# Projections with the bias in the weights' last row, and reciprocal roots by Newton steps on GpSimd

## The chip, the cores and the metric

The kernel runs on one core of a Trainium2 chip. The metric is the device time of one execution in microseconds (us); lower is better. PE is TensorE, DVE is VectorE, ACT is ScalarE, POOL is GpSimd, SP is SyncE, which here only issues DMAs.

## The reference, cut to what matters

The program is a whole two-layer model. The change lies in the first part of layer 0, a normalization, a feed-forward block on its result, and the projections of a recurrent attention:

```python
hs = layernorm(x)                       # 4096 tokens x 128; mean 0 over the 128 features
q = silu(hs @ Wq + bq)                  # 128 -> 16 heads x 64; the same for k and v
g = hs @ Wg + bg                        # 128 -> 1024, with silu
beta = sigmoid(hs @ Wb + bb)            # 16 heads; 4 more gates alike
q = q * rsqrt(sum(q * q, axis=-1) + 1e-6)   # per token and head; the same for k
```

The q, k and v that leave this stage are scaled per token and head: q and k by their reciprocal norms, k and v also by the root of beta.

## The kernel before, in words

The kernel is written engine by engine; each engine's instructions run in the order written, and semaphores order them between engines. Phases end with `end_phase`, where every engine waits for every other.

**Load stage and feed-forward block (0 to 203 us).** SP issues the loads. Those counted by `ld2` are the gate weights `wgate`, gate biases, small constants, the projection bias `bias_p` and the four weight matrices `wproj` (L1533 to L1539). DVE normalizes all 4096 tokens at once (L507 to L516), with `xnT` as scratch space, quantizes the result and the weights (L581 to L593), and then works through 16 pairs of token tiles. PE turns each tile of `xn`, ACT copies it to `xnT` (`keep_x`, L2077), and from there the gate logits are formed (L1811, L1814). POOL clears `bias3` and splits the bias into three bf16 parts (L1674 to L1681), which go through DRAM into three rows of `bias3`.

**Projections (203 to 506 us).** There are 32 tiles of 128 tokens, each with 4096 outputs in 8 PSUM banks. Per tile i:

- PE computes for each bank the f32 product (L1858) and adds the bias by a bf16 matmul of ones with the three bias rows (L1859). It reuses a bank when ACT has read the same bank of tile i-1.
- ACT evicts each bank through Silu (L2124), and squares q after bank 2 and k after bank 4 (L2130, L2133). After bank 2 it also takes the roots of the 32 sums of the tile before (L2128).
- DVE sums the squares per head (L2320, L2332), takes the reciprocals of the roots of tile i-1 (L2317) and multiplies q, k and v of tile i-1 in place by `prj_f`, one instruction on 128x3072 (L2325).
- POOL squares v (L1699) and multiplies the factors of k by the root of beta (L1693).
- SP stores the finished tile, 2 MB, to `proj_s` (L1556). `prj` has four slots, and ACT waits for the store of tile i-4.

DVE's order in turn i is: reciprocal (i-1), sum of q (i), multiply (i-1), sum of k (i), sum of v (i). The quotes from the other engines stand below.

Of the kernel before, what the change touches and what calls it, by code (L numbers as in the profile page):

```python
# [42 lines left out]
ROUNDER = 1.5 * 2 ** 22  # L43
TIES_DOWN = 1.0 - 2.0 ** -22
# [26 lines left out]
def layer_kernel(nc, a, out):  # L71

    ctx = ExitStack()
    with ctx:
        def sem(name):
            return ctx.enter_context(nc.semaphore(name))
# [21 lines left out]
        bias_s = nc.dram_tensor("bias_s", (3, 4 * HD), BF16, kind="Internal").ap()  # L98
# [32 lines left out]
        above_fa = sb("above_fa", [P, T * D], scope=s1)  # L131
# [15 lines left out]
        ones3 = sb("ones3", [P, P], BF16, scope=sW)  # L147
# [12 lines left out]
        bias3 = sb("bias3", [P, 4 * HD], BF16, scope=s2)  # L160
# [206 lines left out]
        v_prj = sem("v_prj")  # L367
        p_normed = sem("p_normed")
# [109 lines left out]
        bias_split, bias_out, bias_in, b_summed = bias_sems  # L478
# [25 lines left out]
        def layernorm(dve, c, src, dst, turned, layer):  # L504
# [11 lines left out]
            c.link(dve.tensor_tensor(dst[:, :, :], dst[:, :, :], rstd.unsqueeze(2).to_broadcast([P, T, D]), ALU.mult))  # L516

# [1004 lines left out]
        def _(sp):  # L1522
# [142 lines left out]
        def _(pool):  # L1665
# [11 lines left out]
            split.link(pool.tensor_copy(bias_h[:, 0, :], bias_p[:, :]))  # L1677
            split.link(pool.tensor_tensor(bias_r[:, 0, :], bias_p[:, :], bias_h[:, 0, :], ALU.subtract))
            split.link(pool.tensor_copy(bias_h[:, 1, :], bias_r[:, 0, :]))
            split.link(pool.tensor_tensor(bias_r[:, 1, :], bias_r[:, 0, :], bias_h[:, 1, :], ALU.subtract))  # L1680
            split.done(pool.tensor_copy(bias_h[:, 2, :], bias_r[:, 1, :]))  # L1681
# [8 lines left out]
            for i in range(T + 1):  # L1690
                if i >= 1:
                    pool.wait_ge(v_prj, i + 1)
                    pool.tensor_tensor(prj_f[:, i - 1, H0:2 * H0], prj_f[:, i - 1, H0:2 * H0], sb_tok[:, i - 1, :], ALU.mult).then_inc(p_sq, 1)  # L1693
                if i < T:
                    pool.wait_ge(p_silu, 8 * i + 6)
                    if i:
                        pool.wait_ge(p_red, 3 * i)
                    x = prj[:, i % 4, 2 * HD:3 * HD]
                    pool.tensor_tensor(prj_sq[:, 2, :], x, x, ALU.mult).then_inc(p_sq, 1)  # L1699
# [72 lines left out]
        def _(pe):  # L1772
# [32 lines left out]
            def gate_logits(p):  # L1805

                if p == 0:
                    pe.wait_ge(ld2, 144)
# [254 lines left out]
        def _(act):  # L2063
# [9 lines left out]
            def keep_x(p):  # L2073
# [3 lines left out]
                act.copy(xnT[:, 2 * P * p:2 * P * p + 2 * P], bank[0][:, 0:2 * P]).then_inc(xT_done, 1)  # L2077
# [40 lines left out]
            for i in range(T + 1):  # L2118
                if i < T:
                    if i >= 4:  # L2120
                        act.wait_ge(p_stored[i % 4], 16 * (i // 4))
                    for n in range(8):
                        act.wait_ge(p_mm, 8 * i + n + 1)
                        act.activation(prj[:, i % 4, 512 * n:512 * n + 512], bank[n], ACT.Silu).then_inc(p_silu, 1)  # L2124
                        if n == 2:
                            if i:
                                act.wait_ge(p_red, 3 * i - 1)
                                act.activation(prj_n[:, (i - 1) % 2, 1, :], prj_n[:, (i - 1) % 2, 0, :], ACT.Sqrt, bias=prj_eps[:, 0:1]).then_inc(p_std, 1)  # L2128
                            act.wait_ge(p_silu, 8 * i + 2)
                            act.activation(prj_sq[:, 0, :], prj[:, i % 4, 0:HD], ACT.Square).then_inc(p_sq_q, 1)  # L2130
                        if n == 4:
                            act.wait_ge(p_silu, 8 * i + 4)
                            act.activation(prj_sq[:, 1, :], prj[:, i % 4, HD:2 * HD], ACT.Square).then_inc(p_sq_q, 1)  # L2133
            act.wait_ge(p_red, 3 * T - 1)
            act.activation(prj_n[:, (T - 1) % 2, 1, :], prj_n[:, (T - 1) % 2, 0, :], ACT.Sqrt, bias=prj_eps[:, 0:1]).then_inc(p_std, 1)
# [117 lines left out]
        def _(dve):  # L2253
# [25 lines left out]
            for p in range(FP):  # L2279
# [8 lines left out]
                if p == FP - 2:  # L2288
                    dve.wait_ge(g_raw, 2 * FP)
                    dve.tensor_tensor(sb_tok[:, :, :], sb_tok[:, :, :], beta_row[:, 0:2 * H0:2].unsqueeze(1).to_broadcast([P, T, H0]), ALU.add).then_inc(b_summed, 1)  # L2290
                    dve.wait_ge(ld2, 144)
# [17 lines left out]
            pv_ = Count(dve, p_var)  # L2309
            for i in range(T + 1):  # L2310
# [4 lines left out]
                if i >= 1:  # L2315
                    dve.wait_ge(p_std, i)
                    prc.link(dve.reciprocal(prj_f[:, i - 1, 0:2 * H0], prj_n[:, (i - 1) % 2, 1, :]))  # L2317
                if i < T:
                    dve.wait_ge(p_sq_q, 2 * i + 1)
                    dve.tensor_reduce(prj_n[:, i % 2, 0, 0:H0], prj_sq[:, 0, :].rearrange("p (h d) -> p h d", d=DK), AX, ALU.add).then_inc(p_red, 1)  # L2320
                if i >= 1:
                    t = i - 1
                    dve.wait_ge(p_sq, 2 * i)
                    qkv3 = prj[:, t % 4, 0:3 * HD].rearrange("p (h d) -> p h d", d=DK)
                    dve.tensor_tensor(qkv3, qkv3, prj_f[:, t, :].unsqueeze(2).to_broadcast([P, 3 * H0, DK]), ALU.mult).then_inc(p_normed, 1)  # L2325
                if i < T:
                    for w, dst in ((1, prj_n[:, i % 2, 0, H0:2 * H0]), (2, vv[:, i, :])):
                        if w == 1:
                            dve.wait_ge(p_sq_q, 2 * i + 2)
                        else:  # L2330
                            dve.wait_ge(p_sq, 2 * i + 1)
# [284 lines left out]
```

## Time and profile before

| | |
|---|---|
| three runs | 3071.02 us median (3070.17 to 3073.48) |
| profiled execution | 3071.01 us |
| its span in the trace | 3069.2 us |
| load stage and feed-forward block | 0 to 203 us |
| projections | 203 to 506 us |
| busy of the span: PE, DVE, ACT, POOL | 86%, 75%, 52%, 45% |
| busy in 200 to 506 us: PE, DVE, ACT, POOL | 289, 234, 286, 92 us |

A busy share over the whole span mixes stages with different limits; for this change the stage of the projections and the load stage before it are to be read by themselves. The page's chain of work that ended last holds only about a fifth of the span and does not reach back to these stages. Spans on POOL are rough.

### The profile page before, as it was taken

To read this page: it belongs to the slowest core of one execution; us is meant where nothing else is said; L and a number is where in the kernel's file an instruction comes from. 1 tells how busy PE (TensorE), PEld (TensorE's weight loads), DVE (VectorE), ACT (ScalarE), POOL (GpSimd) and SP (SyncE) were. 2 spreads that over 40 slices of the span, in tenths; PEclk is the share of its full clock that TensorE was granted. 3 is DMA by queue.
4 is the path that set the end of the run, shared out by engine and by line. 5 is a ranking of instruction groups with operands and counts; after the bars stand their busy time and mean duration, and the time that the engine had idled before them with its cause. 6 is when DMAs were issued, how large, how long until landed. Compare 5 with 4: busy or idle time off the path is not lost. (4 is left out here: it accounts for less than half of the span.)

```text
span 3069.2 us, 68844 instructions
## 1 busy us (share of the span) xinstructions
PE 2648.2 (86%) x24613; PEld 1773.4 (58%) x24613; DVE 2313.0 (75%) x4183; ACT 1602.5 (52%) x4014; POOL 1367.1 (45%) x2167
## 2 busy tenths in 40 slices
PE   0889996749999999999999999999573988888888
PEld 0654443637777777777777777777472932222223
DVE  8868887956868688786878878765786477877775
ACT  0459996853434444444444444444582645555555
POOL 1113233115756667676666757666555024211111
PEclk9989997978999999999999999999797979999999
DMA  2016656862242333224233322321684212111110
GB/s 63 1 69 241 242 246 250 251 193 45 41 89 67 61 70 81 55 61 88 67 61 70 81 53 63 81 67 49 239 275 141 76 32 39 25 28 25 22 22 28
DMA packets 459979, 288.37 MB, mean 94 GB/s; under 512 B 375251, under 2 KB 419859, under 8 KB 450835
## 3 DMA queue, kind: packets, MB, share of 16 engines
q1 hardware_dynamic: 450422, 254.56, 30.4%
q10 hardware_dynamic: 4608, 16.78, 1.8%
q0 software_dynamic: 4608, 12.59, 1.2%
q8 instruction: 201, 3.29, 0.5%
q14 instruction: 140, 1.15, 0.1%
HBM read 153.83 MB, written 129.99 MB: 92 GB/s over the span
## 5 line engine op out<-in xcount | busy, mean ns | idle before, releaser
L2535 DVE TENSOR_REDUCE mx<-banks 128x2 f32<-128x1024 f32 (+3 forms) x384 | 358.2, 956 | 106.7 <-PE banks L1979 84.3
L2240 ACT ACTIVATE probs<-banks 128x1024 f32<-128x1024 f32 (+3 forms) x384 | 307.1, 811 | 245.9 <-PE banks L2001 238.9
L1765 POOL TENSOR_SCALAR_AFFINE_SELECT probs<-probs 128x256 f32<-128x256 f32 x256 | 103.7, 407 | 524.9 <-ACT probs L2240 524.7
L874 POOL TENSOR_SCALAR xc<-xc,halves 128x64 f32<-128x64 f32 (+1 forms) x256 | 150.6, 588 | 268.4 <-DVE xc L1379 255.5
L1858 PE MATMUL banks<-wproj,xnT 128*128 128x512 f32 x512 | 264.7, 599 | 0.6 <-DVEq L497 0.6
L1180 ACT COPY ssm<-banks 16x64 f32<-16x64 f32 (+2 forms) x896 | 216.7, 242 | 50.1 <-PE banks L977 37.9
L1227 ACT COPY ah<-banks 128x768 f32<-128x768 f32 x128 | 102.3, 799 | 254.5 <-PE banks L1050 254.5
L1050 PE MATMUL banks<-stk,tw 128*128 128x192 f32 x1024 | 204.7, 344 | 0.5 <-DVE tw L1385 0.5
L2001 PE MATMUL banks<-q_less,k_parts 64*128 64x512 bf16 (+3 forms) x768 | 133.6, 345 | 80.9 <-DVE mx L2535 59.9
L2018 PE MATMUL banks<-probs,vaug 128*9 128x256 f32 (+3 forms) x1920 | 196.1, 450 | 0.0
L1218 ACT ACTIVATE nycv<-banks 128x512 f32<-128x512 f32 x128 | 76.5, 598 | 207.4 <-PE banks L1040 207.4
L1040 PE MATMUL banks<-S_t,kqt 64*128 64x128 f32 x2048 | 184.1, 298 | 0.0
L881 POOL TENSOR_TENSOR ag<-ah,gt_sb 128x512 f32<-128x512 f32 x128 | 164.2, 1283 | 36.9 <-ACT ah L1227 32.7
L1050 PEld LDWEIGHTS banks<-stk,tw 128*128 128x128 f32 x1024 | 166.3, 193 | 16.2 <-DVE tw L1385 0.7
L1194 ACT COPY xs<-banks 128x128 f32<-128x128 f32 x128 | 34.1, 266 | 265.3 <-PE banks L1010 265.3
L1858 PEld LDWEIGHTS banks<-wproj,xnT 128*128 128x128 f32 x512 | 96.3, 191 | 98.2 <-issue 48.4
L1065 PE MATMUL banks<-nycv,ah 128*128 128x128 f32 x1024 | 148.3, 288 | 0.0
L977 PE MATMUL banks<-kqt 64*128 64x256 f32 x1024 | 147.3, 407 | 0.0
L1699 POOL TENSOR_TENSOR prj_sq<-prj 128x1024 f32<-128x1024 f32 x32 | 77.5, 2421 | 148.7 <-ACT prj L2124 148.7
L1979 PE MATMUL banks<-k_parts,q_parts 64*128 64x512 bf16 (+3 forms) x768 | 136.1, 350 | 6.6 <-DVE mx L2535 3.0
L1072 PE MATMUL banks<-qkv_t,ag 128*128 128x64 f32 x1024 | 141.4, 281 | 0.0
L1040 PEld LDWEIGHTS banks<-S_t,kqt 64*128 64x128 f32 x2048 | 134.9, 187 | 10.5
(368 smaller groups left out, 6762.2 us busy)
## 6 DMA issues: line engine op xcount, KB each, us to landing
proj_s<-prj SPq DMA_DIRECT2D x32, 2048.0 KB, 6.8
qkv_t<-proj_s SPq DMA_DIRECT2D x32, 1536.0 KB
ka<-proj_s ACTq DMA_DIRECT2D x32, 512.0 KB, 4.9
mem_s<-o_sb SPq DMA_DIRECT2D x32, 512.0 KB, 2.7
om<-mem_s SPq DMA_DIRECT2D x32, 512.0 KB, 4.0
om<-proj_s SPq DMA_DIRECT2D x32, 512.0 KB, 4.9
nblk_s<-ssa POOLq DMA_DIRECT2D x32, 256.0 KB, 4.4
blk_s<-res SPq DMA_DIRECT2D x16, 512.0 KB, 4.2
```

The lines of the kernel that those rows point to most:

```text
L874: pool.tensor_scalar(inverse_of(k, lv + 1)[:, :, w:2 * w], inverse_of(k, lv), halves[:, lv, 1:2], None, ALU.mult).then_inc(half_set, 1)
L881: pool.tensor_tensor(ag[:, :, :], ah[:, k % 2, :, 0:P], gt_sb[:, k % 2, :, :], ALU.mult).then_inc(ag_set, 1)
L977: last = pe.matmul(bk[m % 2][:, 256 * p:256 * p + 256], kqt[r, k % 2, p, 0, :], kqt[r, k % 2, p, :, :].rearrange("p w t -> p (w t)"), star ...
L1040: last = pe.matmul(cols(bk[2 + m % 2], 2 * w + p), kqt[r, k % 2, p, w, :], S_t[r, 2 * g + p, :], start=(w == 0 and p == 0), stop=(w == 0), ...
L1050: last = pe.matmul(cols(bk[p], m % 2, P + DK), tw[:, k % 2, m, :], stk[:, k % 2, m, :], start=True, stop=True)
L1065: last = pe.matmul(cols(bk[2 + m % 2], 2 + p), ah[:, k % 2, m, 0:P], nycv[:, k % 2, m, 0:P], start=False, stop=True, skip_group_check=True)
L1072: last = pe.matmul(cols(bk[2 + m % 2], p, DK), ag[:, m, :], qkv_t[:, n, 2 * HD + DK * h:2 * HD + DK * h + DK], start=True, stop=True)
L1180: last = act.copy(dst, both[rows, :, :, right])
L1858: pe.matmul(bank[n], xnT[:, P * i:P * i + P], wproj[:, 512 * n:512 * n + 512], start=True, stop=False)
L2018: last = pe.matmul(bank[6][row:row + SLOT, n0 * P:512], vaug[:, b * TB + j, 2 * (s % 8) + e, :], p_, start=(j == 0), stop=(j == 6 + odd))
L2240: act.activation(probs[:, s % 2, :, at:at + w], slot_of((kind, s, k))[:, :, 0:w], ACT.Exp, scale=D1 ** -0.5).then_inc(b_read, 1)
L2535: dve.tensor_reduce(mx[:, s % 2, c, :, t:t + 1].rearrange("p e a -> p (e a)"), slot_of((kind, s, k))[:, :, 0:w], AX, ALU.max).then_inc(a_r ...
```

## The change

The features of a normalized token sum to zero. So the last row of each weight matrix can be subtracted from all its rows without changing the product; the last row is then zero, and its place is taken by the bias, against a last row of `xnT` that is held at 1. SP loads the last rows as broadcasts (`wlast`, `wglast`) and POOL subtracts them. The bf16 bias matmul, the split of the bias and its way through DRAM are gone.

The roots on ACT and the reciprocals on DVE are gone too. DVE adds 1e-6 to the sums, forms a first value of the reciprocal root from the bits of the number, and POOL refines it with three Newton steps of four linked instructions on 128x32. DVE's order in turn i becomes: sum of q (i), sum of k (i), first value (i), multiply (i-1), sum of v (i). POOL's becomes: square of v (i), Newton steps (i), multiply by the root of beta (i).

```diff
+LD2 = 16 * 13
+ROOT_BITS = 0x5F3759DF
 sync
-            sp.dma_start(bias_p[:, :], a["bproj"].rearrange("a (p n) -> (a p) n", p=P)).then_inc(ld2, 16)
+            sp.dma_start(wglast[:, :], a["wgate"][D - 1:D, :].rearrange("a n -> (a n)").partition_broadcast(P)).then_inc(ld2, 16)
             for n, w in enumerate(("Wq", "Wk", "Wv", "Wg")):
                 sp.dma_start(wproj[:, HD * n:HD * n + HD], a[w]).then_inc(ld2, 16)
-            sp.wait_ge(bias_split, 5)
-            sp.dma_start(bias_s.rearrange("c (p n) -> p c n", p=P), bias_h[:, :, :]).then_inc(bias_out, 16)
-            sp.wait_ge(bias_out, 16)
-            sp.wait_ge(bias_set, 2)
-            sp.dma_start(bias3[0:3, :], bias_s).then_inc(bias_in, 16)
+            for n, w in enumerate(("Wq", "Wk", "Wv", "Wg")):
+                sp.dma_start(wlast[:, HD * n:HD * n + HD], a[w][D - 1:D, :].rearrange("a n -> (a n)").partition_broadcast(P)).then_inc(ld2, 16)
+            sp.wait_ge(w_centred, 2)
+            sp.dma_start(wproj[D - 1:D, :], a["bproj"]).then_inc(bias_in, 16)
 gpsimd, load stage
-            pool.memset(ones3[:, :], 1.0).then_inc(bias_set, 1)
-            pool.wait_ge(xq_done, 1)
-            pool.memset(bias3[:, :], 0.0).then_inc(bias_set, 1)
-            pool.wait_ge(ld2, 144)
-            split = Count(pool, bias_split)
...
+            pool.wait_ge(ld2, LD2)
+            pool.tensor_tensor(wgate[:, :], wgate[:, :], wglast[:, :], ALU.subtract).then_inc(w_centred, 1)
+            pool.tensor_tensor(wproj[:, :], wproj[:, :], wlast[:, :], ALU.subtract).then_inc(w_centred, 1)
+            pool.wait_ge(w_centred, 2)
+            pool.wait_ge(norm_done, 1)
+            pool.memset(xnT[3 * P // 4:P, :], 1.0).then_inc(xone_set, 1)
+            pool.wait_ge(xone_set, 1)
 gpsimd, projections
+            root = Count(pool, p_std)
+            pool.wait_ge(v_prj, 1)
+            for i in range(T):
+                n, v = i % 2, prj[:, i % 4, 2 * HD:3 * HD]
+                pool.wait_ge(p_silu, 8 * i + 6)
+                if i:
+                    pool.wait_ge(p_red, 3 * i)
+                pool.tensor_tensor(prj_sq[:, 2, :], v, v, ALU.mult).then_inc(p_sq, 1)
+                pool.wait_ge(seeded, 2 * i + 2)
+                total, norm, y = prj_n[:, n, 0, :], prj_n[:, n, 1, :], prj_f[:, i, 0:2 * H0]
+                for _ in range(3):
+                    root.link(pool.tensor_tensor(total, y, y, ALU.mult))
+                    root.link(pool.tensor_tensor(total, total, norm, ALU.mult))
+                    root.link(pool.tensor_scalar(total, total, -0.5, 1.5, ALU.mult, ALU.add))
+                    root.link(pool.tensor_tensor(y, y, total, ALU.mult))
+                pool.tensor_tensor(prj_f[:, i, H0:2 * H0], prj_f[:, i, H0:2 * H0], sb_tok[:, i, :], ALU.mult).then_inc(v_prj, 1)
 tensor
-                    pe.matmul(bank[n], xnT[:, P * i:P * i + P], wproj[:, 512 * n:512 * n + 512], start=True, stop=False)
-                    pe.matmul(bank[n], ones3[:, :], bias3[:, 512 * n:512 * n + 512], start=False, stop=True).then_inc(p_mm, 1)
+                    pe.matmul(bank[n], xnT[:, P * i:P * i + P], wproj[:, 512 * n:512 * n + 512], start=True, stop=True).then_inc(p_mm, 1)
 scalar, keep_x
+                if p == 0:
+                    act.wait_ge(xone_set, 1)
+                act.copy(xnT[0:D - 1, 2 * P * p:2 * P * p + 2 * P], bank[0][0:D - 1, 0:2 * P]).then_inc(xT_done, 1)
 scalar, projections
+                    if n in (2, 4):
+                        w = n // 2 - 1
+                        act.wait_ge(p_silu, 8 * i + n)
+                        if i:
+                            act.wait_ge(p_red, 3 * i - 2 + w)
+                        act.activation(prj_sq[:, w, :], prj[:, i % 4, HD * w:HD * w + HD], ACT.Square).then_inc(p_sq_q, 1)
 vector, projections
+                if i < T:
+                    for w in range(2):
+                        dve.wait_ge(p_sq_q, 2 * i + w + 1)
+                        dve.tensor_reduce(prj_n[:, i % 2, 0, H0 * w:H0 * w + H0], prj_sq[:, w, :].rearrange("p (h d) -> p h d", d=DK), AX, ALU.add).then_inc(p_red, 1)
+                    norm, y = prj_n[:, i % 2, 1, :], prj_f[:, i, 0:2 * H0]
+                    dve.wait_ge(p_red, 3 * i + 2)
+                    seed.link(dve.tensor_scalar(norm, prj_n[:, i % 2, 0, :], 1e-6, None, ALU.add))
+                    dve.tensor_scalar(y.bitcast(I32), norm.bitcast(I32), -0.5, ROOT_BITS, ALU.mult, ALU.add).then_inc(seeded, 1)
+                    seed.n += 1
                 if i >= 1:
                     t = i - 1
+                    dve.wait_ge(v_prj, t + 2)
+                    dve.wait_ge(p_sq, t + 1)
```

The v sum of tile i stays behind the multiply. PE's gate logits and the later readers wait for `w_centred` and the larger `ld2` count.

## Rows read from the trace of the kernel before

**Rows 1.** Windows in the projections: length, busy (instructions) per engine, PE clock, DMA, GB/s.
```profile
300.00:400.00 100.00, 100.00 (x275) 42.88 (x274) 81.55 (x57) 99.33 (x148) 29.16 (x22) 1.00 0.64 242
```
**Rows 2.** Groups by line and shape, 200 to 500 us: busy us, mean ns | idle before.
```profile
L2124 ACT ACT_TABLE_LOAD x32 | 41.1, 1283 | 6.7 <-PE banks L1859 6.2
L2332 DVE TENSOR_REDUCE vv<-prj_sq 128x16 f32<-128x1024 f32 x32 | 39.0, 1220 | 21.5 <-POOL prj_sq L1699 21.5
```
**Rows 3.** Timeline, 300 to 320 us: start us, us, engine, line, operation.
```profile
299.70 1.02 PE L1858 MATMUL banks<-wproj,xnT 128*128 128x512 f32 x2
300.56 0.38 PE L1859 MATMUL banks<-bias,ones 128*128 128x512 bf16 x1
301.28 3.35 DVE L2325 TENSOR_TENSOR prj<-prj,prj_f 128x3072 f32<-128x3072 f32 x1
303.27 3.04 ACT L2124 ACTIVATE prj<-banks 128x512 f32<-128x512 f32 x6
303.94 2.43 POOL L1699 TENSOR_TENSOR prj_sq<-prj 128x1024 f32<-128x1024 f32 x1 [4.17 <-ACT prj L2124]
310.13 3.35 DVE L2325 TENSOR_TENSOR prj<-prj,prj_f 128x3072 f32<-128x3072 f32 x1
```
**Rows 4.** Two lines' instructions: count, duration ns min/median/max, first and last start.
```profile
L1699 POOL TENSOR_TENSOR prj_sq<-prj x32: 1893/2430/2680, 212.9 to 489.8; 128x1024 f32<-128x1024 f32 x32
L2325 DVE TENSOR_TENSOR prj<-prj,prj_f x32: 3347/3349/3358, 221.6 to 494.2; 128x3072 f32<-128x3072 f32 x32
```
**Rows 5.** Timeline of the bias split, 63 to 69 us, POOL and DVE.
```profile
64.64 2.15 DVE L582 TENSOR_SCALAR fsc<-fsc 128x70 f32<-128x70 f32 x1
66.99 0.24 POOL L1678 TENSOR_TENSOR bias_r<-bias_p,bias_h 128x32 f32<-128x32 f32 x1
67.30 0.21 POOL L1679 CAST bias_h<-bias_r 128x32 bf16<-128x32 f32 x1
67.45 1.32 DVE L584 SCALAR_TENSOR_TENSOR fa<-wraw,fsc 128x1120 f32<-128x1120 f32 x1
67.59 1.29 POOL L1680 TENSOR_TENSOR bias_r<-bias_r,bias_h 128x32 f32<-128x32 f32 x1
```
**Rows 6.** Short POOL instructions of the later chunk stage: timeline, then by line.
```profile
1011.00 1.82 POOL L857 TENSOR_TENSOR bx<-bx,bt 128x24 f32<-128x24 f32 x1
1011.01 1.72 DVE L1283 TENSOR_TENSOR res<-res 128x900 f32<-128x900 f32 x1
...
L856 POOL TENSOR_SCALAR bx<-bt,rf_abs x256: 316/317/555, 706.8 to 2143.2; 128x12 f32<-128x12 f32 x128
L857 POOL TENSOR_TENSOR bx<-bx,bt x128: 232/234/1830, 707.6 to 2143.6; 128x24 f32<-128x24 f32 x128
L874 POOL TENSOR_SCALAR xc<-xc,halves x256: 442/602/2025, 693.2 to 2137.0; 128x64 f32<-128x64 f32 x128
```
**Rows 7.** Load stage: timeline, a window from 14 us, and Wg's issue (KB, us to landing).
```profile
13.59 0.43 SPq L1539 DMA_DIRECT2D wproj<-in_Wg  x1
28.75 0.18 DVE L513 TENSOR_SCALAR stats<-stats 128x32 f32<-128x32 f32 x1
29.62 4.43 DVE L516 TENSOR_TENSOR xn<-xn,stats 128x4096 f32<-128x4096 f32 x1
...
14.00:19.00 5.00, 0.00 (x0) 0.00 (x0) 4.93 (x3) 0.00 (x0) 0.00 (x0) 1.00 0.98 389
...
wproj<-in_Wg SPq DMA_DIRECT2D x1, 512.0 KB, 6.3
```
**Rows 8.** Timeline of the projections' end.
```profile
493.86 0.22 POOL L1693 TENSOR_TENSOR prj_f<-prj_f,sb_tok 128x16 f32<-128x16 f32 x1 [1.59 <-DVE prj_f L2317]
494.02 5.86 POOL L1701 MEMSET gl<- 128x6912 f32 x1
494.19 3.36 DVE L2325 TENSOR_TENSOR prj<-prj,prj_f 128x3072 f32<-128x3072 f32 x1 [0.40 <-POOL prj_f L1693]
```
**Rows 9.** A window with gaps on PE (the tenth column is the clock).
```profile
2120.00:2160.00 40.00, 28.24 (x303) 22.09 (x301) 21.68 (x46) 10.16 (x35) 18.91 (x33) 0.86 0.03 10
```

More of the change, by code:

```diff
@@ L130, in layer_kernel @@
         fa = sb("fa", [P, T * D], scope=s1)
-        above_fa = sb("above_fa", [P, T * D], scope=s1)
+        wlast = sb("wlast", [P, 4 * HD], scope=s1)
         fsc = sb("fsc", [P, 2, T * D // BLOCK], scope=s1)
@@ L159, in layer_kernel @@
         s2 = ExitStack()
-        bias3 = sb("bias3", [P, 4 * HD], BF16, scope=s2)
+        below_sq = sb("below_sq", [P, 2 * HD], scope=s2)
         prj_sq = sb("prj_sq", [P, 3, HD], scope=s2)
@@ L367, in layer_kernel @@
         v_prj = sem("v_prj")
+        seeded = sem("seeded")
         p_normed = sem("p_normed")
@@ L477, in layer_kernel @@
         bias_sems = [updated, mixed, squared, ratio_set]
-        bias_split, bias_out, bias_in, b_summed = bias_sems
+        w_centred, xone_set, bias_in, b_summed = bias_sems
         ffn_sems = [staged, x_turned, xT_done, gu_done, silu_done, hid_done]
@@ L1671, in _ @@
                                pattern=[[-1, P]], channel_multiplier=1).then_inc(const_set, 1)
-            pool.memset(ones3[:, :], 1.0).then_inc(bias_set, 1)
-            pool.wait_ge(xq_done, 1)
-            pool.memset(bias3[:, :], 0.0).then_inc(bias_set, 1)
-            pool.wait_ge(ld2, 144)
-            split = Count(pool, bias_split)
[L1677 to L1681, printed above, removed]
+            pool.wait_ge(ld2, LD2)
[5 more added lines that the diff above has]
+            pool.wait_ge(xone_set, 1)
             for p in range(FP):
@@ L1689, in _ @@
                 pool.sem_clear(x).then_inc(cleared, 1)
[L1690 to L1699, printed above, removed]
+            root = Count(pool, p_std)
[14 more added lines that the diff above has]
+                pool.tensor_tensor(prj_f[:, i, H0:2 * H0], prj_f[:, i, H0:2 * H0], sb_tok[:, i, :], ALU.mult).then_inc(v_prj, 1)
             pool.wait_ge(p_silu, 8 * T)
@@ L1807, in gate_logits @@
                 if p == 0:
-                    pe.wait_ge(ld2, 144)
+                    pe.wait_ge(w_centred, 1)
                 else:
@@ L2076, in keep_x @@
                 act.copy(xqT[:, :, :].rearrange("p y w -> p (y w)"), bank[0][:, 2 * P:4 * P]).then_inc(xT_done, 1)
-                act.copy(xnT[:, 2 * P * p:2 * P * p + 2 * P], bank[0][:, 0:2 * P]).then_inc(xT_done, 1)
+                if p == 0:
+                    act.wait_ge(xone_set, 1)
+                act.copy(xnT[0:D - 1, 2 * P * p:2 * P * p + 2 * P], bank[0][0:D - 1, 0:2 * P]).then_inc(xT_done, 1)
             def gate(p):
@@ L2117, in _ @@
             act.wait_ge(cleared, len(prj_sems))
[L2118 to L2135, printed above, removed]
+            for i in range(T):
+                if i >= 4:
+                    act.wait_ge(p_stored[i % 4], 16 * (i // 4))
+                for n in range(8):
+                    act.wait_ge(p_mm, 8 * i + n + 1)
+                    act.activation(prj[:, i % 4, 512 * n:512 * n + 512], bank[n], ACT.Silu).then_inc(p_silu, 1)
+                    if n in (2, 4):
[4 more added lines that the diff above has]
+                        act.activation(prj_sq[:, w, :], prj[:, i % 4, HD * w:HD * w + HD], ACT.Square).then_inc(p_sq_q, 1)
             act.wait_ge(g_stored, 16)
@@ L2290, in _ @@
                     dve.tensor_tensor(sb_tok[:, :, :], sb_tok[:, :, :], beta_row[:, 0:2 * H0:2].unsqueeze(1).to_broadcast([P, T, H0]), ALU.add).then_inc(b_summed, 1)
-                    dve.wait_ge(ld2, 144)
+                    dve.wait_ge(ld2, LD2)
                     dve.tensor_tensor(bgate[:, 2:3], bgate[:, 0:1], bgate[:, 1:2], ALU.add).then_inc(g_bias, 1)
@@ L2299, in _ @@
             seq.link(dve.tensor_reduce(bmask[:, :], ident[:, :].rearrange("p (h j) -> p j h", j=NB), AX, ALU.add))
-            dve.wait_ge(ld2, 144)
+            dve.wait_ge(ld2, LD2)
             dve.scalar_tensor_tensor(out=rf_abs[:, :], in0=rf_c[:, :], scalar=-1.0, in1=rf_c[:, :], op0=ALU.mult, op1=ALU.max).then_inc(rf_set, 1)
             seq.link(dve.tensor_scalar(one_rf[:, :], rf_c[:, :], 1.0, None, ALU.add))
-            dve.memset(prj_eps[:, :], 1e-6).then_inc(bias_set, 1)
-            dve.wait_ge(bias_set, 3)
             dve.wait_ge(sb_root, 1)
@@ L2308, in _ @@
             prc.link(dve.tensor_copy(prj_f[:, :, 2 * H0:3 * H0], sb_tok[:, :, :]))
-            pv_ = Count(dve, p_var)
+            pv_, seed = Count(dve, p_var), Count(dve, seeded)
             for i in range(T + 1):
@@ L2326, in _ @@
                 if i < T:
[L2327 to L2331, printed above, removed]
-                        dve.tensor_reduce(dst, prj_sq[:, w, :].rearrange("p (h d) -> p h d", d=DK), AX, ALU.add).then_inc(p_red, 1)
+                    dve.wait_ge(p_sq, i + 1)
+                    dve.tensor_reduce(vv[:, i, :], prj_sq[:, 2, :].rearrange("p (h d) -> p h d", d=DK), AX, ALU.add).then_inc(p_red, 1)
             dve.wait_ge(p_red, 3 * T)
```

12 lines of the change are left out of this document (1 added, 11 removed).

## The prediction

> **What bounds the kernel now.** I read the page's slices first: the edited loop is the stretch from 203 to 506 us, and the page's chain of waits does not reach back to it, so the bound is read from windows and the timeline. In 300 to 400 us PE is busy all 100 us and ACT 99.33; DVE has 81.55 and POOL only 29.16 [rows 1]. Among ACT's work are 32 table loads of 1.283 us before a Silu [rows 2], and as many before the small roots. The timeline gives the period: the big DVE multiply L2325 starts at 301.28 and 310.13, 8.85 us apart [rows 3]. PE needs for a bank 0.86 us for the f32 pair (starts 299.70 and 300.56) [rows 3] and then the bias matmul. PE and ACT, both without idle time, bound the stage, and the change relieves both. The question is who is next.
>
> **What goes.** PE: 8 bias matmuls a tile; it is left with 8 x 0.86 = 6.9 us. ACT: two table loads, 2 x 1.28 = 2.6 us a tile, and a root; left at most 6.3. That the loads go rests on row 303.27: six Silus follow a Square with no load between [rows 3]. DVE: one reciprocal on 128x32.
>
> **What comes.** DVE gets two seeds on 128x32. Such a TENSOR_SCALAR took 0.18 us (L513) [rows 7], so with the wait between them 0.4. DVE a tile is then 3.35 + 3 x 1.22 + 0.4 + gaps of 0.1 = 7.5 us [rows 2]. POOL gets 12 linked steps on 128x32, each waiting for the one before, then the multiply by the beta root.
> - A tensor_tensor step: the bias split has the same shape, L1678 took 0.24 and the next instruction started 0.31 us after it [rows 5]. The gap after the next one is 0.08 (67.30 + 0.21 to 67.59). I take 0.25 + 0.08 = 0.33, nine times: 2.97.
> - A tensor_scalar step with two constants is in no row. Below: the CAST of 128x32, 0.21, step 0.29 [rows 5]. Above: 128x64 at its median of 0.602, step 0.69. Nearest are 128x12 at 0.317 and 128x64 at least 0.442 [rows 6]; between them 128x32 is 0.317 + 20/52 x 0.125 = 0.365, step 0.45, three times: 1.35.
> - Last multiply 128x16: 0.22 (L1693, start 493.86) [rows 8].
> Newton in all: 2.97 + 1.35 + 0.22 = 4.54 us. Alone that would be harmless: with the V square of 1.89 POOL has 6.4 us.
>
> **The collision.** POOL instructions that read SBUF and the DVE multiply with two SBUF operands do not run together. L1699 takes 1.893 us at least, but 2.430 in the median [rows 4]: at 303.94 it starts 0.69 before the multiply ends (304.63), and ends 1.74 after that end [rows 3]. L1680, 128x32, took 1.29 instead of 0.24 beside DVE's L584, which began 0.14 earlier; L857, 128x24, took 1.82 instead of a median of 0.234 beside L1283 [rows 5, 6]. A POOL memset, which reads nothing, ran from 494.02 beside the multiply and left it alone (3.36) [rows 8]. The reductions read one tensor; beside them nothing is stretched.
> So each tile the 3.35 us multiply stands in POOL's queue as if POOL ran it, unless POOL is idle then. It won't be: after Newton(i-1) POOL goes straight to square(i), whose waits (Silu of V, reduction i-1) are long met, then to Newton(i); the multiply (i-1) is released only by the end of Newton(i-1), so it always falls among these. Overlap at the joint saves 0.14 (1.89 - 1.75, from rows 3 and 4). Period = 1.89 + (3.35 - 0.14) + 4.54 = **9.64 us** against 8.85. DVE (7.5), PE (6.9), ACT (6.3) and the store (2 MB at 237 to 242 GB/s now) are below that. Behind the multiply on DVE wait reductions and seeds of the next tile, 4.2 us; they end before Newton does (4.54 after the multiply), so they add nothing.
>
> **Sum for the projections.** First multiply: tile 0's Newton is hidden behind tile 1's squares, but square(1) on POOL comes first; I place its start 0.5 us later than 221.6. Then 30 periods: 30 x 0.79 = 23.6. The last interval is 3.35 - 0.14 + 4.54 + 0.11 = 7.86 against 7.1 now (first to last start is 272.6, less 30 x 8.85) [rows 4]: 0.8. What follows the last multiply, store and end of stage (506.5), is the same. Sum **+24.9**.
>
> **The load stage.** ld2 now includes four broadcasts of 512 KB and a small one. Wg's issue is at 13.59 and it lands 6.3 later, 19.9 [rows 7]; 2 MB more at the 389 GB/s moved while these weights came [rows 7] is 5.4 us: about 25.3. Then POOL subtracts 128x80 and 128x4096. Slope from L1693 and L1699: (1.893 - 0.221)/1008 = 1.66 ns an element, so 0.3 + 7.0 us, to about 32.6. DVE has a tensor_scalar at 28.75 and a two-operand multiply at 29.62 [rows 7], and the whole stage up to 203 us hangs on that DVE chain. It waits until about 32.6: 32.6 - 28.93 = +3.7. The bounds are +2 (the loads land earlier, or only the second multiply is held) and +7 (they land as it is about to start). In return the old bf16 memset goes, beside which L582 took 2.15 us; the like L513 took 0.18: -2.0 [rows 5, 7]. Net **+1.7** (0 to 5). The memset of xnT waits for the normalization, only writes, and is done by 43 us, long before ACT's copy at 79; the bias row's DMA is far from the 203 us at which it is wanted. SP issues five loads more and two fewer at about 0.45, which no one waits for except ld2.
> The trace's slope disagrees with the Trainium skill, page "GPSIMD Engine Reference", section "3.1 Elementwise — side-by-side cycle accounting", which gives about 2.6 cycles an element for a two-input tensor_tensor, so by its figures an estimate of 9 us for this subtraction; the sum would be 2 us higher. The measured slope stands.
>
> **Total.** The profiled execution took 3071.01 us with a span of 3069.2; the median is 3071.02, so no correction. 3071 + 24.9 + 1.7 = 3097.6, **3098 us**.
>
> **Rivals.**
> - A, the forecast, 62%. Its own range: all tensor_scalar steps at the CAST price and the others at 0.31 give Newton 3.91, a period of 9.01, +5.4, and with 1.7 in the load stage 3078; two-constant steps at 0.69 give Newton 5.26, a period of 10.4, 30 x 1.51 + 2 = +47, and 3120. As the step values from rows lie nearer the middle: 3080 to 3114.
> - B, break-even, 6%. The load stage and the two ends cost about 2, so the period must fall to 8.79, Newton to 3.7 us, 0.29 a step: just under the cheapest linked steps of rows 5. It gives 3065 to 3077.
> - C, the collision does not bind, 18%: the multiply slips into POOL's waits (ACT or the seeds may arrive late in a way I don't see) or short POOL steps pass beside it. Then DVE bounds, 7.65 us: 30 x -1.2 = -36, +1.7: **3037**, faster. For it: DVE's multiply was never stretched (3.347 to 3.358) [rows 4]. Against it: every overlap with a multiply in [rows 3, 5, 6] stretches POOL. That the table loads don't go changes nothing here, as ACT at 8.85 would still be below 9.64.
> - D, dearer POOL steps, 10%: if every step costs what the shortest tensor_scalar of 128x64 does, 0.442 + 0.08 [rows 6], Newton is 12 x 0.52 + 0.22 = 6.5, the period 11.6 and the time 3071 + 30 x 2.7 + 3 + 2 = **3157**; half of that way 3127.
> - E, the clock, 4%. PE will idle 2.7 us a tile, where it now has none and is granted 1.00 (2.4 GHz) [rows 1]. In 2120 to 2160, where it has gaps, it was granted 0.86 [rows 9]. At 1.2 GHz throughout, a bank is 1.71 and a tile 13.7: 32 x 4.85 = +155, 3226. A partial drop as at 2120 (6.9/0.86 = 8.0) stays under 9.64. The Trainium skill, page "TensorE: Matmul & The Clock Gate", section "A second HAM failure mode: psum-queue depth-cycling", says that a PE which idles briefly between groups of matmuls while cycling through PSUM banks loses throughput to a clock that oscillates; this is that pattern.
>
> **Numbers.** A change under 0.2% (6 us) can't be told from none. Slower: A, D, E, 76%, and a quarter of B: 77%. Within 0.2%: most of B and a little of C, 6%. Faster: 17%. Range 3068 to 3117: below lies C, above most of D and E, together about a quarter, of which D's mild half reaches in again.
>
> **What the new profile must show.** (1) POOL idle nearly nowhere in the loop; starts of L2325 9.6 us apart. At 7.6 C holds. (2) In each tile one POOL instruction stretched by 3.2 us, or the multiply stretched by a square in flight. (3) Tensor_tensor steps 0.33 and tensor_scalar steps 0.45 apart. (4) No table load in the loop, f32 matmul pairs 0.86 apart, ACT near 65% busy. (5) A DVE instruction at 28.75 or 29.62 stretched by about 3.7, L582 on wraw short. The forecast is wrong if POOL waits for seeds or for ACT, or if its small steps run at their own length beside the multiply.

## The result and the profile after the change

| | before | after |
|---|---|---|
| time, median of 7 runs (range) | 3071.18 us (3066.97 to 3073.48) | 3086.22 us (3079.23 to 3089.39) |
| ratio, with its 95% interval | 1 | 1.0045 (1.0033 to 1.0058) |
| profiled execution: time, span | 3071.01, 3069.2 | 3086.22, 3084.5 |
| period of the projections' loop | 8.85 us a tile | 9.06 us a tile |
| loop, first to last start of the multiply | 272.6 us | 280.25 us |
| start of the mask's reduction (`bmask`, DVE), just ahead of the projections | 205.05 us | 212.29 us |
| MEMSET of cc (DVE's first instruction of the next stage) | 506.51 us | 521.35 us |

The kernel is 15 us slower. The forecast was 3098, with 3068 to 3117 as its range. The last rows of the table place the loss: 7.2 us are there before the projections begin, 7.7 arise in the loop, and behind it nothing more than 0.5. The forecast had put 1.7 in the first place and 24.9 in the second.

Windows of the kernel after (length, busy and instructions of PE, PEld, DVE, ACT and POOL, PE's clock, DMA share, GB/s), against [rows 1]:
```profile
300.00:400.00 100.00, 80.87 (x177) 31.58 (x176) 95.97 (x67) 65.93 (x112) 89.18 (x155) 1.00 0.64 237
```
PE fell from 100 to 81 and ACT from 99 to 66 (near 65 was forecast). DVE (96) and POOL (89, its gaps between linked instructions not counted) took their place.

Groups of the kernel after, 200 to 540 us (busy us, mean ns | idle before):
```profile
L2327 DVE TENSOR_TENSOR prj<-prj,prj_f 128x3072 f32<-128x3072 f32 x32 | 154.3, 4822 | 6.5 <-POOL prj_f L1704 3.5
L1700 POOL TENSOR_TENSOR prj_n<-prj_f 128x32 f32<-128x32 f32 x96 | 116.7, 1215 | 6.0 <-DVE prj_f L2320 1.0
L1701 POOL TENSOR_TENSOR prj_n<-prj_n 128x32 f32<-128x32 f32 x96 | 24.7, 257 | 7.5
L1702 POOL TENSOR_SCALAR prj_n<-prj_n 128x32 f32<-128x32 f32 x96 | 20.9, 218 | 8.4
L2129 ACT ACT_TABLE_LOAD x1 | 1.3, 1283 | 5.7 <-PE banks L1863 5.7
```
Three things to see. The big multiply, 3349 ns in the median before [rows 4], now has a mean of 4822 for the same shape. L1700 is listed at 1215 ns, its twin L1701 at 257, for the same shape: one execution in three of L1700 is stretched. And of 32 table loads before a Silu [rows 2] one is left.

Timeline of the kernel after (start us, us, engine, line, operation), against [rows 3]; first a tile in which the multiply comes before POOL's square, then one in which the square comes first. The second order is the rule: 28 of the 32 multiplies last 5.03 us. The first tile shown is the only one in which a square is held up (the group of squares has a mean of 1988 ns); the other three unstretched multiplies are the first one and two of the last three.
```profile
299.76 3.36 DVE L2327 TENSOR_TENSOR prj<-prj,prj_f 128x3072 f32<-128x3072 f32 x1
299.84 5.03 POOL L1696 TENSOR_TENSOR prj_sq<-prj 128x1024 f32<-128x1024 f32 x1
304.83 0.24 POOL L1700 TENSOR_TENSOR prj_n<-prj_f 128x32 f32<-128x32 f32 x1
...
308.71 0.25 POOL L1704 TENSOR_TENSOR prj_f<-prj_f,sb_tok 128x16 f32<-128x16 f32 x1
308.93 1.89 POOL L1696 TENSOR_TENSOR prj_sq<-prj 128x1024 f32<-128x1024 f32 x1
308.94 7.34 PE L1863 MATMUL banks<-wproj,xnT 128*128 128x512 f32 x16 [1.93 <-ACT prj L2129]
309.00 5.03 DVE L2327 TENSOR_TENSOR prj<-prj,prj_f 128x3072 f32<-128x3072 f32 x1
310.78 3.35 POOL L1700 TENSOR_TENSOR prj_n<-prj_f 128x32 f32<-128x32 f32 x1
314.21 0.25 POOL L1701 TENSOR_TENSOR prj_n<-prj_n 128x32 f32<-128x32 f32 x1
314.55 0.22 POOL L1702 TENSOR_SCALAR prj_n<-prj_n 128x32 f32<-128x32 f32 x1
314.85 0.25 POOL L1703 TENSOR_TENSOR prj_f<-prj_f,prj_n 128x32 f32<-128x32 f32 x1
315.18 0.24 POOL L1700 TENSOR_TENSOR prj_n<-prj_f 128x32 f32<-128x32 f32 x1
```
In the first tile the square waits for the whole multiply: 5.03 = 1.89 + 3.14 us. In the second the multiply waits for the square in flight, 5.03 = 3.35 + 1.68, and then it holds POOL's first Newton step for 3.1 us (3.35 against 0.24). The two square starts are 9.09 apart, and the order makes no difference to that: POOL has the square, the multiply and the Newton steps one after the other either way.

### The profile page after: what moved, and what is told of

It reads as the page before. It is cut to its first block and busy times, and to the rows that moved or that the text cites. A ratio compares the mean times of both kernels' runs of the same rounds, so it can differ in the third digit from the quotient of the medians.

```text
span 3084.5 us, 68715 instructions
## 1 busy us (share of the span) xinstructions
PE 2602.6 (84%) x24357; PEld 1748.3 (57%) x24357; DVE 2370.8 (77%) x4214; ACT 1515.1 (49%) x3920; POOL 1546.7 (50%) x2547
## 3 DMA queue, kind: packets, MB, share of 16 engines
q8 instruction: 199, 3.26, 0.5%
## 5 line engine op out<-in xcount | busy, mean ns | idle before, releaser
L1863 PE MATMUL banks<-wproj,xnT 128*128 128x512 f32 x512 | 233.7, 607 | 41.9 <-ACT prj L2129 41.4
L2327 DVE TENSOR_TENSOR prj<-prj,prj_f 128x3072 f32<-128x3072 f32 x32 | 154.3, 4822 | 6.5 <-POOL prj_f L1704 3.5
```

## Experiments

Each kernel ran beside runs of the kernel before on the same chip; its ratio is to those. Besides the time, two markers of the trace are used: the period (distance of two starts of the multiply) and the MEMSET of cc (506.51 us before, 521.35 after).

**Two Newton steps for three.** The factors are then less exact.
```
-                for _ in range(3):
+                for _ in range(2):
```


> The changed kernel with two Newton steps instead of three, so the factors are less exact; nothing else differs. Theory P (the period of 9.06 us is POOL's own work plus the multiply that stands in its way, 1.89 + 3.1 + 4.1): four linked instructions less, 1.29 us a tile, so the period falls to between 7.8 and 8.15 (at 8.15 the square on POOL holds up DVE's first values, which are then due at the same time), and the time to 3050 to 3059. Rival D (DVE is the bound: it is 97% busy and its multiply lasts 5.03 us): nothing is taken from DVE, the period stays 9.06 and the time 3086.

Measured: 3051.02 us (3049.34 to 3052.81), ratio 0.9936 (0.9919 to 0.9952), period 8.02, MEMSET of cc at 485.85. A third of the steps carries 35 us. From its timeline:
```profile
304.57 1.89 POOL L1696 TENSOR_TENSOR prj_sq<-prj 128x1024 f32<-128x1024 f32 x1
305.36 1.13 DVE L2319 TENSOR_SCALAR prj_n<-prj_n 128x32 f32<-128x32 f32 x1
306.62 3.35 DVE L2327 TENSOR_TENSOR prj<-prj,prj_f 128x3072 f32<-128x3072 f32 x1
306.79 3.28 POOL L1700 TENSOR_TENSOR prj_n<-prj_f 128x32 f32<-128x32 f32 x1 [0.33 <-DVE prj_f L2320]
```
The square now meets the seed (the first value, formed by DVE on 128x32), which ends with it: 1.13 instead of 0.18 us. DVE is busy 99.17 of 100 us here, so it has become the bound: POOL's own sum would be 9.06 - 1.29 = 7.77, and DVE's is its unstretched 7.07 (the next two runs) plus these 0.95, 8.02. POOL still pays the multiply on one 128x32 step.

**No Newton steps.** The factors are only their first values.
```
-                for _ in range(3):
+                for _ in range(0):
```


> The changed kernel with no Newton step at all: the factors are the first values, so the scaling is inexact. Theory P: POOL has 2.1 us of its own; the square comes before the first values are formed and meets nothing, DVE alone sets the period, 7.07 us as with the one-operand instruction: about 3025 (3086 less 30 x 2.0). Rival Q: the square itself collides each tile with the first values or the multiply, and the period stays near the 8.02 us of two steps.

Measured: 3024.16 us (3017.00 to 3026.16), ratio 0.9843 (0.9822 to 0.9863), period 7.07. From its timeline:
```profile
302.02 2.34 DVE L2316 TENSOR_REDUCE prj_n<-prj_sq 128x16 f32<-128x1024 f32 x2
302.25 1.89 POOL L1696 TENSOR_TENSOR prj_sq<-prj 128x1024 f32<-128x1024 f32 x1 [1.20 <-ACT prj L2129]
304.70 3.35 DVE L2327 TENSOR_TENSOR prj<-prj,prj_f 128x3072 f32<-128x3072 f32 x1
304.87 3.26 POOL L1704 TENSOR_TENSOR prj_f<-prj_f,sb_tok 128x16 f32<-128x16 f32 x1 [0.73 <-DVE prj_f L2320]
```
The collision is still in every tile, on L1704 (3.26 for 0.25), and costs nothing: POOL has 0.73 us of idle time before it and 1.20 before the square. It needs a full POOL queue to cost something. And 7.07 is DVE's own period, its instructions back to back.

**The multiply with one operand from SBUF.** The scaling is left out: a reduction over the same 128x3072 stands in its place, with as long a duration (3346 ns).
```
-dve.tensor_tensor(qkv3, qkv3, prj_f[:, t, :].unsqueeze(2).to_broadcast([P, 3 * H0, DK]), ALU.mult).then_inc(p_normed, 1)
+dve.tensor_reduce(prj[:, t % 4, 0:3 * H0], qkv3, AX, ALU.add).then_inc(p_normed, 1)
```


> The changed kernel with DVE's multiply on 128x3072 (two SBUF operands) replaced by a sum over the same 3072 elements (one operand, 48 results into the same tile), so the scaling of q, k and v is left out. DVE's time for it should be the same 3.3 us. Theory P (the two operands collide with POOL's reads): no POOL instruction is stretched any more, POOL needs 6.1 us a tile, and DVE's 7.5 to 7.9 us set the period: about 3044 to 3056. Rival L (the loop is a chain of waits between DVE and POOL, and the port has no part in it): all waits are unchanged, the period stays at 9.06 and the time at 3086.

Measured: 3027.15 us (3022.89 to 3029.51), ratio 0.9855 (0.9838 to 0.9871), period 7.07. Its groups, 200 to 540 us:
```profile
L2327 DVE TENSOR_REDUCE prj<-prj 128x48 f32<-128x3072 f32 x32 | 107.1, 3346 | 0.0
L1700 POOL TENSOR_TENSOR prj_n<-prj_f 128x32 f32<-128x32 f32 x96 | 23.1, 241 | 29.6 <-DVE prj_f L2320 24.6
```
This is the run that shows the cause. DVE is as long at work as before, all waits stand, POOL has the same 13 instructions a tile and the square, and in the steady loop no instruction of either is stretched (near its start two of DVE's first values are, near its end one square and one DVE product on 128x448): L1700 is at 241 ns for 1215, and POOL waits for DVE. So it was the multiply itself, and neither its duration nor a chain of waits. The edit takes away two things at once, the second SBUF operand and most of the results (48 written for 3072). Two rows of the kernel after tell them apart:
```profile
124.55 1.39 POOL L595 TENSOR_TENSOR hq<-fa,fsc 128x704 f32<-128x704 f32 x1 [5.25 <-DVE fa L590]
124.72 0.88 DVE L2272 TENSOR_TENSOR hid<-silu_g,banks 128x704 f32<-128x704 f32 x1
```
Here a DVE tensor_tensor writes 704 results beside a POOL instruction that reads SBUF, but one of its inputs comes from PSUM (`banks`). L2272 and L595 run so side by side in 14 of their 16 turns, and neither is ever longer than 0.89 and 1.39 us. That leaves the second SBUF operand. The time went below its expectation (3044 to 3056) because DVE's own period is 7.07 and not 7.5.

**V's square on ACT.** All of the reference is computed.
```
-                pool.wait_ge(p_silu, 8 * i + 6)
-                if i:
-                    pool.wait_ge(p_red, 3 * i)
-                pool.tensor_tensor(prj_sq[:, 2, :], v, v, ALU.mult).then_inc(p_sq, 1)
...
+                    if n == 6:
+                        act.wait_ge(p_silu, 8 * i + 6)
+                        if i:
+                            act.wait_ge(p_red, 3 * i)
+                        act.activation(prj_sq[:, 2, :], prj[:, i % 4, 2 * HD:3 * HD], ACT.Square).then_inc(p_sq, 1)
```


> The changed kernel with the square of V on ACT, after bank 6, instead of POOL. Theory P: POOL keeps 4.1 for the Newton steps and 3.1 for the multiply, 7.2 us, so DVE's 7.6 us set the period: 30 x -1.45 = -43, about 3043. Rival A (ACT then waits for DVE's V sum in the middle of its bank order and holds PE up): the period is 8.2 or more and the time over 3060.

Measured: 3029.34 us (3025.23 to 3032.95), ratio 0.9859 (0.9842 to 0.9875), periods 7.20 and 7.35. Its window and group:
```profile
300.00:400.00 100.00, 98.55 (x225) 41.75 (x224) 98.31 (x82) 93.84 (x153) 84.36 (x181) 1.00 0.75 291
...
L2328 DVE TENSOR_TENSOR prj<-prj,prj_f 128x3072 f32<-128x3072 f32 x32 | 108.2, 3382 | 4.2 <-POOL prj_f L1700 2.5
```
1.89 us less on POOL is worth 53 to 57 us against the changed kernel (3082.57 and 3086.22, its two medians); 43 were expected, with DVE's period taken as 7.6. Each Newton chain still carries one stretched step, but POOL has the time for it, and the multiply meets nothing longer than 0.25 us (3382 ns). All four engines lie between 84 and 99%. DVE (98.31) and POOL are level here: in every other tile the multiply starts only as POOL's L1700 ends (306.07 and 306.03), in the others POOL waits 0.33 for DVE.

**The Newton part alone**, with the bias matmuls and the loads of before:


> The kernel before with the roots' part alone (first value on DVE, three Newton steps on POOL, no roots on ACT); bias matmuls stay. Theory P: POOL's 9.06 us a tile is above PE's 8.6, so the loop is as in the changed kernel, 7.7 us longer in all, and the load stage as before: 3079. Rival M (bias matmuls on PE matter beside it, since ACT now waits for DVE in one stretch and PE must catch up): a period of 9.3 or more, over 3085.

Measured: 3078.56 us (3074.35 to 3082.57), ratio 1.0023 (1.0012 to 1.0034), period 9.04, MEMSET of cc at 515.68 (+9.2, of which 7.1 arise between the first and the last multiply and 2.2 before the first). PE is busy 99.74 of 100 us there: with the bias matmuls still in it, it has hardly a gap, and the period is that of the whole change. The loop's loss is this part's, and taking the matmuls away gives it nothing back.

**The weights part alone**, with the roots of before:


> The kernel before with the weights' part of the change alone (bias in the last row, subtraction on POOL, no bias matmuls); roots and reciprocals stay on ACT and DVE. The theory that ACT bounds the loop of before at 8.85 us: PE's relief brings nothing, the load stage costs its 6 to 8 us, 3077 to 3079. Rival B (PE and ACT bound it together, so that a freer PE shortens ACT's waits): the loop falls by up to 0.3 us a tile and the time is 3068 to 3073.

Measured: 3073.08 us (3065.06 to 3081.13), ratio 1.0002 (0.9988 to 1.0016), period 8.85.
```profile
300.00:400.00 100.00, 83.34 (x183) 32.76 (x182) 80.69 (x58) 99.33 (x148) 29.89 (x23) 1.00 0.65 247
```
PE has 17% to spare, ACT is where it was (99.33), and the period with it: of the 8 matmuls saved in each tile nothing comes back. The mask's reduction starts at 210.54 (+5.5), the first multiply at 224.79 (+3.2: from that reduction on, the first tile is 2.3 us quicker), and the MEMSET of cc at 509.68 (+3.2). The median is below the 3077 to 3079 of the expectation, at the edge of what rival B gave; what decides against B is the loop, 272.57 us from first to last multiply as before (272.58).

**The changed kernel again**, timed beside the next:


> The changed kernel itself, beside the other kernels of this set, since the two halves of the change alone gave +1 and +6 us and PE's centring gave 14 us where the trace shows 8 in its stage. If the parts add up (theory), it takes 3079 to 3083 here; if the first timing stands (rival: the two parts together cost more than alone), 3085 or more.

Measured: 3082.57 us (3077.72 to 3086.66), ratio 1.0037 (1.0023 to 1.0050), period 9.03 to 9.04, MEMSET of cc at 518.73. The markers add up: +3.2 and +9.2 for the parts, +12.2 for the whole. The medians (+1, +6, +10, each against the kernel before beside it) do so within their scatter.

**The subtraction behind the normalization.** Same instructions, another place in POOL's queue.
```
+            pool.wait_ge(norm_done, 1)
             pool.tensor_tensor(wproj[:, :], wproj[:, :], wlast[:, :], ALU.subtract).then_inc(w_centred, 1)
             pool.wait_ge(w_centred, 2)
-            pool.wait_ge(norm_done, 1)
```


> The changed kernel with POOL's subtraction on the four weight matrices held back until DVE has normalized the tokens. It then begins beside a one-operand reduction of 4.41 us and is 8.81 us long. Theory S (only DVE instructions that use the shared port wait): the reduction is not stretched, the tensor_scalar after it (L584, 0.29 us) lasts until the subtraction ends, 4.5 us late instead of 7.9, and the time is 3 us below the changed kernel's. Rival W (any DVE work beside it waits, or the wait is one for memory): the reduction is stretched too and nothing is gained.

Measured: 3079.29 us (3071.25 to 3085.09), ratio 1.0025 (1.0015 to 1.0036), 3.3 below the changed kernel beside it, a difference that the two intervals do not separate. First the load stage of the changed kernel, then this one's:
```profile
24.16 4.42 DVE L511 TENSOR_REDUCE stats<-xnT 128x32 f32<-128x4096 f32 x1
27.40 0.35 POOL L1674 TENSOR_TENSOR wgate<-wgate,wglast 128x80 f32<-128x80 f32 x1 [24.63 <-DMA wlast<-in_Wg]
27.71 8.81 POOL L1675 TENSOR_TENSOR wproj<-wproj,wlast 128x4096 f32<-128x4096 f32 x1
28.62 7.94 DVE L512 TENSOR_SCALAR stats<-stats 128x32 f32<-128x32 f32 x1
37.24 4.42 DVE L515 TENSOR_TENSOR xn<-xn,stats 128x4096 f32<-128x4096 f32 x1
```
```profile
33.99 4.41 DVE L583 TENSOR_REDUCE fsc<-xn 128x256 f32<-128x4096 f32 x1
34.15 8.83 POOL L1676 TENSOR_TENSOR wproj<-wproj,wlast 128x4096 f32<-128x4096 f32 x1 [6.46 <-DVE stats L2257]
38.43 4.69 DVE L584 TENSOR_SCALAR fsc<-fsc 128x256 f32<-128x256 f32 x1
```
In the changed kernel a DVE instruction of 0.18 us stands still for 7.9, until POOL's ends at 36.5, and all of the stage with it. Moved, the subtraction lies half beside a reduction, which keeps its 4.41, and only a DVE tensor_scalar of 0.29 is held, for 4.4. The gain of 3.4 that this makes is there where PE begins the feed-forward block (76.84 for 80.22 and, in the second profile of the changed kernel, 80.05), but not at the mask's reduction (210.63 for 210.93): in between, in 96 to 102 us, this execution was granted a clock of 0.57, and the fourth copy to `xnT` comes 11.5 us after the third, where it is 8.9 in the second profile.

**The subtraction on PE.** A matrix (the identity with a last row of -1) multiplies the weights, ACT copies the result back; the four broadcast loads and POOL's 128x4096 go. All is computed.
```
+            for n in range(8):
+                pe.matmul(bank[n], cen, wproj[:, 512 * n:512 * n + 512], start=True, stop=True).then_inc(cen_mm, 1)
...
+            for n in range(8):
+                act.wait_ge(cen_mm, n + 1)
+                act.copy(wproj[:, 512 * n:512 * n + 512], bank[n]).then_inc(cen_kept, 1)
...
-            pool.tensor_tensor(wproj[:, :], wproj[:, :], wlast[:, :], ALU.subtract).then_inc(w_centred, 1)
```


> The changed kernel with the last row subtracted from the four weight matrices by PE (a matrix of ones on the diagonal and minus ones in its last row, eight f32 matmuls and eight copies by ACT, while both are idle) instead of by POOL; the four broadcast loads are gone. The projections are untouched. Theory S (the 8.81 us subtraction on POOL blocked DVE's tensor_scalar L512 for 7.94 us in the load stage, and the whole stage hangs on DVE): L512 is back at 0.2 us, the stage ends 7 us earlier, 3079. Rival T (the stage's 7 us are from the copies' waits and the TensorE clock after it, or PE's and ACT's new work delays the transposes): 3084 or more.

Measured: 3072.34 us (3069.14 to 3080.84), ratio 1.0008 (0.9998 to 1.0018). From its load stage, and its first 220 us as a window:
```profile
21.47 2.85 POOL L1681 TENSOR_TENSOR wgate<-wgate,wglast 128x80 f32<-128x80 f32 x1 [17.67 <-DMA wproj<-in_Wg]
21.53 8.84 PE L1789 MATMUL banks<-wproj,wlast 128*128 128x512 f32 x16 [21.53 <-DMA wproj<-in_Wg]
28.59 0.18 DVE L514 TENSOR_SCALAR stats<-stats 128x32 f32<-128x32 f32 x1
28.94 3.98 ACT L2083 COPY wproj<-banks 128x512 f32<-128x512 f32 x8
...
0.00:220.00 220.00, 129.50 (x632) 94.83 (x633) 172.08 (x205) 70.41 (x150) 35.81 (x43) 0.83 0.13 38
```
The 7.8 us stall is gone (0.18), as the theory of the port wanted, and PE begins the feed-forward block 7.7 to 7.9 us earlier (72.35). The mask's reduction, at 206.17, has 4.8 to 6.1 left of it. The mean clock of 0.83 (0.95 in the changed kernel) is not the measure of that loss, as it is low mostly where PE has nothing to do; what costs is a short stretch:
```profile
32.00:72.00 40.00, 0.00 (x0) 0.00 (x0) 39.30 (x20) 0.93 (x2) 3.51 (x1) 0.54 0.00 0
90.00:96.00 6.00, 5.07 (x13) 3.56 (x14) 5.37 (x9) 1.61 (x3) 1.15 (x2) 0.50 0.01 3
```
There the fourth copy to `xnT` again comes 11.5 us after the third. The last run below has the same subtraction on PE and a mean of 0.84 in its first 220 us, but 1.00 in 90 to 96, and it keeps all of the gain: its mask's reduction starts at 202.86, 8.1 before that of the changed kernel's second profile. The median here is back at that of the kernel before, 10 to 14 us below the changed kernel, which is more than the 7 expected and more than this trace shows (MEMSET of cc at 514.33, 4.4 to 7.0 earlier).

**Both repairs together** (V's square on ACT, the subtraction on PE), all computed:


> The changed kernel with both edits: V's square on ACT, and PE instead of POOL subtracting the last row of the four weight matrices. Theory P and S together: the loop as in the run with V's square on ACT (periods of 7.20 to 7.36 us, 3029) and the load stage 7.8 us shorter: about 3020, below the kernel before by 1.6 to 1.7%. Rival: the two are not independent, the loop starts at another phase or clock, and it stays at 3025 or more.

Measured: **3020.31 us (3016.44 to 3025.97), ratio 0.9834 (0.9816 to 0.9852)**. Periods 7.20 and 7.36, MEMSET of cc at 458.50. It is the fastest kernel here that computes the factors as exactly as the changed one: 52 us below the kernel before beside it, 62 to 66 below the changed kernel.

**Both, with two Newton steps:**


> As the one with both edits, and with two Newton steps instead of three (less exact factors). Theory P: with three steps POOL's 4.1 + 3.1 = 7.2 us is as long as DVE's own 7.07; with two it is 5.9, so only DVE is left, periods 7.07: 4 us less than with three, about 3016. Rival D (DVE alone sets 7.2 to 7.36): no difference.

Measured: 3011.49 us (3010.92 to 3019.31), ratio 0.9809 (0.9789 to 0.9830), period 7.07, DVE 99.03% busy. Less exact for 9 us, where 4 were expected: 7.0 of the 9.0 at the MEMSET of cc (449.47) arise in the loop, 1.4 before the mask's reduction. Here DVE alone is the bound, and the 0.13 to 0.29 a tile that three steps cost more are POOL's.

## Why the prediction came out as it did

**The mechanism was right.** The forecast's case was A: POOL becomes the bound because DVE's multiply stands in its queue as if POOL ran it. The larger of POOL's sum (with the multiply in it) and DVE's own holds in each run that changed a term: two steps (8.02, DVE's 7.07 and a stretched first value), the square moved (7.20 to 7.36, both level), one operand (7.07, no stretch), no steps (7.07, stretch but no cost). Rival C, 7.65 us because the multiply slips through, did not come about: it needs a POOL with spare time, and the runs with spare time are just those at 7.1 to 7.4. D fell (a step of 0.30 to 0.34), and so did E: PE idles 19 of 100 us and is granted 1.00. What was cited for E, from the Trainium skill, "TensorE: Matmul & The Clock Gate", section "A second HAM failure mode: psum-queue depth-cycling", did not show: the page has it from a bf16 kernel, and in this f32 loop the cycling through eight banks cost no clock. One premise was half right: PE and ACT were both named as the bound of before, but with PE relieved alone (83.34) the period stays 8.85, so ACT by itself set it. It changed nothing in the sum.

**The total was 12 us too high because two terms erred in opposite directions.** The loop was put 17.2 us too high, the load stage 5.5 too low; that the sum came so near is in part luck.

*The loop, +24.9 forecast, +7.7 measured.* The period was put at 9.64 and is 9.06:
- Newton 4.54, measured 4.10, from 304.83 to the start of the next square at 308.93. The term that was mis-sized is the tensor_scalar with two constants: interpolated between 128x12 and the shortest 128x64 [rows 6] at 0.365 with a step of 0.45, it takes 0.218 with a step of 0.30. Three times 0.15 is all of the difference; the tensor_tensor steps are 0.31 to 0.34, as taken (0.33). Rows of the same operation but other shapes [rows 6] were given more weight than the CAST of the same shape (0.21, step 0.29) in [rows 5], which was right to 0.01.
- The multiply, 3.21, is 3.1 (3.35 less the 0.24 that the step it holds up takes anyway).
- Together some 0.55 a tile of 0.58 (9.64 less 9.06), 17 us in 30 tiles. Of the 7.7 that came, 6.3 are 30 periods of 0.21 and 1.4 the loop's ends. The break-even case B asked for a period of 8.79, only 0.27 below what came: 6% was little for it.

*The load stage, +1.7 forecast, +7.2 measured.* The place and the mechanism were right, and the -2.0 came (the L582 of [rows 5] has 0.20 for 2.15). Two sizes failed:
- POOL's 128x4096 was put at 7.0 us by a slope from 16 to 1024 elements, and took 8.81. The Trainium skill, "GPSIMD Engine Reference", section "3.1 Elementwise — side-by-side cycle accounting", led to an estimate of 9; the trace's slope was preferred to it, and the slope does not reach that far. The page was right here.
- It began at 27.71, not 25.6, as the last load landed at 27.3. Four of the loads' issues took 0.71 to 0.90 us on SP, not 0.45, but that is hardly the reason: Wq, issued before them at 12.00, already landed at 17.7, where it had been 16.1 (12.16 and 3.9), and from 16 to 24 us the loads ran at 398 to 422 GB/s. In 14 to 16 us the DMA engines were as busy as before (0.91 and 0.92) and moved 158 GB/s for 351. With the four broadcasts gone and issues of 0.43 to 0.45 (the subtraction on PE) Wg still lands at 21.4, where it was 19.9. New in both, just ahead of Wq, is the small broadcast `wglast`; that it is the cause was not tried. So DVE is held at 28.62 until 36.5, +7.8 where 3.7 was put. The bound of +7 named for this case was the right reading.
- These two and the -2.0 make +5.7 where PE begins the feed-forward block (80.22 for 74.56). What is left to 7.2 goes with a lower clock in one stretch of that block:
```profile
96.00:102.00 6.00, 3.84 (x13) 2.64 (x14) 5.73 (x9) 1.61 (x3) 1.39 (x1) 0.80 0.00 0
```
The distance of two of its tiles is 8.30 us there, and 6.63 at 1.00 in the second profile of the same kernel, where the mask's reduction starts at 210.93 (+5.9). So the stretch is not in each execution of this kernel. A stretch like it, at 0.50 to 0.80 over 6 us, is in five of the eleven profiles with the change's weights and in neither of the two with the loads of before; whether the change makes it likelier these few can't tell.

**What can be told from the rest.** From the MEMSET of cc to the end, where the kernels are the same, the profiled executions need 2562.7 us (before), 2563.2 (after), 2557.1 (the changed kernel again) and 2566.6 (V's square on ACT); the other nine lie between. So single times differ by up to 9.5 us for no reason in the change, and the markers, not the totals, carry the sums above.

**What stays open:** what makes the short stretches of a lower clock between 90 and 102 us, what makes Wq land 1.6 us later, and why POOL's tensor_tensor costs 1.66 ns an element up to 1024 and (8.81 - 1.89)/3072 = 2.25 from there to 4096. That the square reads one tensor twice is not the reason: L595, with two tensors of 128x704, takes 1.39 us, (1.386 - 0.221)/688 = 1.69.

## What to carry to other kernels

Where DVE has a long instruction with two SBUF operands, charge its duration to POOL's queue too, once for each time POOL is not idle anyway: a stream of short POOL instructions is the worst place to move work to, and moving one of 1.89 us from POOL to an engine with room (here ACT) was worth 53 to 57 us. Work that goes off PE and ACT is worth nothing until the engine that is next has been named with its own sum, and that sum is counted from an unstretched run (7.07), not from busy times added up (7.5). And for a short instruction not in the trace, a row of the same shape can be nearer than rows of the same operation.

## What the runs showed of the hardware beyond that

- Either engine can be the one that waits, and it waits for a whole instruction of the other: DVE's multiply 1.68 us for a POOL square, POOL's 128x32 step 3.1 us for the multiply, a DVE tensor_scalar on 32 elements a partition 7.76 us for a POOL tensor_tensor (7.94 for 0.18). The last one has one tensor operand only, so two SBUF operands are not the whole rule; the forecast counted on it, with "only the second multiply is held" as its lower bound. The reductions, of 128x1024 to 128x4096, were never stretched beside POOL, nor was a tensor_tensor with one of its inputs in PSUM (0.88 us).
- The Trainium skill, "SBUF — State Buffer", section "Who interferes with whom", has both: a port pair that DVE and GpSimd share, held by whichever issues first for its whole instruction, and among those that can want it, besides a tensor_tensor with two SBUF inputs, `tensor_scalar`; `tensor_reduce` never. The runs agree in all three (5.03 for 3.35, 7.94 for 0.18, 4.41 for 4.41). The forecast charged the tensor_scalar its stall, but not the seeds theirs (1.13 with two Newton steps).
- On ACT, Silu and Square ran through the whole loop without a table load between them: one load of 1.283 us at 212.89, before the first Silu, and the next at 494.26, before the gates' root.
- Neighbouring DVE instructions overlap by some 0.1 us in the record: a tile whose durations add up to 7.3 repeats every 7.07.
